# A fused AdaLN block of Mamba-style mixer and routed FFN: half of the next batch's z tiles ahead of the output products, first y statistics behind the state of chunk 6

## The reference, cut to what matters

```python
h = layernorm(x) * (1 + ca) + sa                  # per batch
# mixer, INNER = 512 channels, 8 heads, state 64
xi = silu(causal_conv4(h @ Wx.T));  z = h @ Wz.T
b, c, dt = xi @ Wb.T, xi @ Wc.T, softplus(xi @ Wdt.T + b_dt)
y = ssd_scan(xi, b, c, dt, a) + d * xi            # state carried over 1024 tokens
yn = groupnorm(y)                                 # mean and variance over all tokens of a head
x = x + ga * ((yn * silu(z)) @ Wout.T)            # "output products"
h = layernorm(x) * (1 + cb) + sb
# FFN: router weights h @ rw, the top 127 tokens are gathered, attention and MLP on them,
# scattered back; the others pass through
x = x + gb * ffn(h)
```

## Time and profile before

| | us |
|---|---|
| median of 3 runs | 1397.62 (1397.34 to 1399.22) |
| the profiled execution | 1401.03 |
| its span, first to last instruction | 1399.3 |
| TensorE busy | 1335.8 (95%) |
| VectorE busy | 945.3 (68%) |
| ScalarE busy | 685.8 (49%) |
| GpSimd busy | 351.8 (25%) |

### The profile page before, as it was taken

How to read it: one execution, slowest core, us unless ns; L and a number is a source line. 1 busy time by engine, 2 the same in 40 slices (tenths; PEclk the granted TensorE clock), 3 DMA queues, 4 the chain that set the end, 5 groups by cost and what they waited for, 6 DMA issues and landing times.

```text
span 1399.3 us, 26836 instructions
## 1 busy us (share of the span) xinstructions
PE 1335.8 (95%) x10517; PEld 827.2 (59%) x10531; DVE 945.3 (68%) x2649; ACT 685.8 (49%) x1351; POOL 351.8 (25%) x452
## 2 busy tenths in 40 slices
PE   8999999999999999999999999999999997999984
PEld 4447655586457665586456764576555863567543
DVE  2424797487874787567974878747875779746782
ACT  3534653754546562556436454466526554463312
POOL 3005301171105401072012611053010630134110
PEclk9999999999999999999999999999999998999997
DMA  8100001020000200020010200011000200101010
GB/s 278 45 0 32 9 23 49 1 82 31 27 23 8 75 31 27 23 81 18 14 49 1 82 31 27 23 33 50 30 27 23 81 24 8 49 3 50 31 49 4
DMA packets 47565, 54.47 MB, mean 39 GB/s; under 512 B 7624, under 2 KB 42312, under 8 KB 47440
## 3 DMA queue, kind: packets, MB, share of 16 engines
q1 hardware_dynamic: 41424, 46.41, 9.8%
q0 software_dynamic: 6016, 6.35, 1.7%
HBM read 34.84 MB, written 17.85 MB: 38 GB/s over the span
## 4 chain that ended last, share of the span: by engine, by line
PE 86%; DVE 6%; issue 4%; ACT 1%; DMA 1%; POOL 1%; POOLq 0%; DVEq 0%
PE ps L1576 46%; PE ps L1758 8%; PE ps L1655 4%; PE ps L1701 3%; PE ps L1898 2%; PE ps L1908 2%; PE ps L1667 2%; PE ps L1645 2%; PE ps L1716 1%; PE ps L1673 1%; PE ps L1863 1%; PE ps L1829 1%; PE ps L1684 1%; PE ps L1564 1%; PE ps L1594 1%
## 5 line engine op out<-in xcount | busy, mean ns | idle before, releaser
L1576 PE MATMUL ps<-xT,wb_s 128*128 128x512 f32 x512 | 233.7, 603 | 4.5 <-ACT xT L740 4.4
L1576 PE MATMUL ps<-xT,wc_s 128*128 128x512 f32 x512 | 225.4, 593 | 0.0
L1576 PEld LDWEIGHTS ps<-xT,wc_s 128*128 128x128 f32 x512 | 96.1, 190 | 112.3 <-issue 111.9
L1576 PEld LDWEIGHTS ps<-xT,wb_s 128*128 128x128 f32 x512 | 94.4, 192 | 114.4 <-issue 105.7
L1065 DVE SCALAR_TENSOR_TENSOR xT<-xc,cols_s,xT 128x512 f32<-128x512 f32 x192 | 134.8, 748 | 2.7
L1576 PE MATMUL ps<-hT,wx_s 128*128 128x512 f32 x256 | 117.6, 603 | 0.0
L1576 PE MATMUL ps<-hT,wz_s 128*128 128x512 f32 x256 | 113.8, 598 | 0.1
L1758 PE MATMUL ps<-CT,xT 128*128 128x256 f32 x512 | 111.9, 379 | 0.9 <-DVE xT L1239 0.9
L765 ACT ACTIVATE BT<-ps 128x512 f32<-128x512 f32 x64 | 37.9, 593 | 151.3 <-PE ps L1576 151.3
L1758 PEld LDWEIGHTS ps<-CT,xT 128*128 128x128 f32 x512 | 97.2, 190 | 17.8 <-issue 5.0
L1153 DVE TENSOR_TENSOR Mt<-ps,Eg 128x512 f32<-128x512 f32 x128 | 82.2, 684 | 26.5 <-PE ps L1701 26.5
(11 more groups left out here) (298 smaller groups left out, 2572.4 us busy)
## 6 DMA issues: line engine op xcount, KB each, us to landing
xr<-x SPq DMA_DIRECT2D x8, 1024.0 KB, 10.1
x_scratch<-xr SPq DMA_DIRECT2D x32, 256.0 KB, 2.1
out<-EC SPq DMA_DIRECT2D x32, 256.0 KB, 2.1
BT<-x SPq DMA_DIRECT2D x7, 1024.0 KB, 5.8
modrow<-mod_scratch SPq DMA_DIRECT2D x8, 512.0 KB, 7.0
w_s<-w SPq DMA_DIRECT2D x2, 1024.0 KB, 11.2
BT<-x SPq DMA_DIRECT2D x2, 512.0 KB, 5.4
xT<-wmod SPq DMA_DIRECT2D x1, 1024.0 KB, 9.7
```

What stands on the lines that cost most here:

```text
L1576: ins = t_.matmul(bank[:, :], w[:, k, m * P:(m + 1) * P], rhs[:, k, half * HALF:(half + 1) * HALF], start=k == 0, stop=k == nk - 1)
```

## The change

It has three parts.

- TensorE: the four z tiles of half 0 are issued ahead of `out_(f)` and not behind it. This alters the order for batches 1 to 6.
- ScalarE: the four SiLUs of these tiles are issued ahead of `last_tap(b, 0)`, in batches 0 to 6. In batches 1 to 6 each SiLU of a z tile also waits for the gating of batch b-1 that reads the same part of `zs`.
- VectorE: `y_stats(0, 0, 4)` is issued behind `state(6)` and `skip(6)`, in all eight batches.

```diff
@@ z_silu (ScalarE)
                     act.wait_ge(*proj.full(b, q))
+                    if later(b) and b < NB - 1:
+                        act.wait_ge(gd_ready, at(gd_ready, b - 1, half * KC + m + 1))
                     a.activation(zs[:, m, half * HALF:(half + 1) * HALF], proj.bank(q)[:, :], ACT.Silu
                                  ).then_inc(proj.drained[q % 4], 1)
@@ batch (ScalarE)
-                last_tap(b, 0)
                 if not last:
                     z_silu(b, 0, 0)
-                if not last:
                     z_silu(b, 0, 1)
+                last_tap(b, 0)
                 last_tap(b, 1)
@@ scan (VectorE)
-                    if c == 6:
-                        y_stats(0, 0, 4)
                     if c < T - 1:
                         state(c)
                     else:
                         y_stats(1, 4, 7)
                     skip(c)
+                    if c == 6:
+                        y_stats(0, 0, 4)
                 y_stats(2, 7, 8)
@@ batch (TensorE)
                 x_proj(b, 1, range(4))
                 if f is None:
                     pe.wait_ge(wload, 16 * len(first_loads))
+                if b < NB - 1:
+                    z_proj(b, 0, range(4))
                 if f is not None:
                     out_(f)
                 if b < NB - 1:
-                    z_proj(b, 0, range(4))
                     z_proj(b, 1, range(2))
```

## The result

| | before | after |
|---|---|---|
| median of the runs, us | 1397.62 (1396.32 to 1401.78, 5 runs) | 1432.01 (1429.99 to 1435.27, 5 runs) |
| profiled execution, us | 1401.03 | 1435.27 |
| its span, us | 1399.3 | 1433.5 |
| mean granted clock | 0.985 | 0.983 |

The ratio is 1.0248, 95% interval 1.023 to 1.0266: slower by 34.4 us. The forecast was 1431.4.

A forecast was written before the change was run, and what follows sets the result against it. TensorE was taken to bound the kernel, only 1.66 us above VectorE's chain. Terms 31.3 + 0.6 + 3.2 + 1.7 - 3.0 = +33.8 us on 1397.62 gave 1431.4 us; own range 1427 to 1436, widened to 1422 to 1441.

The forecast's parts named there:

- The floor of 28 us: Output products' end to first C tile: VectorE's chain, 27.99 us in batch 7, was claimed to set it in batches 1 to 6.
- +5.21 us for a batch: Batches 1 to 6: output products end 6.87 us later, the stretch behind them gets 1.66 shorter.
- 31.3 + 0.6: Batches 1 to 6 in all: +31.3 us for the moved z tiles, +0.6 for six bank waits.
- The bank wait: Second z tile reuses an x tile's bank that ScalarE must copy first: 0.1 us a batch, between 0 and 0.6.
- The four waits: TensorE behind the output products: router weights 0.5, first SiLU pair 0.5, B tile at k = 2 2.4, `ffn_idx` 1.4 us.
- no fall: TensorE's clock was taken to stay up behind the new waits, as these are shorter than batch 7's idle stretches.
- the clock rival: Clock falls behind the waits at `ffn_idx`, where nothing hides it: 1.8 us a batch, +10.8, 1442 us; chance 0.11.
- a fall at k = 2 alone: Half clock at the B tile would be hidden: batch 7 had it, 9.80 us against 8.85, within its 27.99.
- The y statistics: `gn_stats` waits for the later statistics, 0.45 us in each of seven batches (0.3 to 0.9): +3.2 us.
- the tail: After batch 7's scan, TensorE resumes 1.75 us earlier and its clock stays up: -3.0 us, between -1.75 and -3.1.
- Batch 0: ScalarE's SiLUs come ahead of the first tap, so the B tile resumes later: +1.7 us, between 0.5 and 3.
- the 0.83 us ahead of the first B tile: Weight load at k = 2 sat idle 0.83 us for ScalarE's last convolved-x SiLU, read as gated by VectorE's chain.

The follow-up runs named there:

- one_tile: Kernel before with one z tile and its SiLU ahead of the output products in batches 1 to 6; 1396.81 us against 1397.73, ratio 0.9993.
- two_tiles: Kernel before with two of the four z tiles and their SiLUs ahead of the output products in batches 1 to 6; 1408.62 us against 1397.73, ratio 1.0064.
- after_filled: Changed kernel with 16 extra products behind the router-weight transposes of batches 1 to 6; 1431.53 us against 1397.09 for the kernel before, ratio 1.0239.
- z_only: Kernel before with the TensorE and ScalarE parts of the change, y statistics left in place; 1432.59 us against 1397.73, ratio 1.0236.
- ystats_only: Kernel before with the VectorE part of the change alone (y statistics moved); 1397.78 us against 1397.73, ratio 1.001.
- before_filled: Kernel before with 16 extra products behind the router-weight transposes of batches 1 to 6; 1418.97 us, ratio 1.0154 to the kernel before.
- ystats_last: Kernel before with the y statistics of chunks 0 to 3 moved in the last batch alone; 1393.94 us against 1397.09, ratio 0.9983.
- silu_swap: ystats_last plus ScalarE's second convolved-x SiLU pair ahead of the last z SiLU pair, batches 1 to 6; 1392.99 us against 1398.28 (kernel before), ratio 0.9964.
- z_last_early: ystats_last plus batch 7's z tiles and SiLUs made as in other batches, dummy products in their old place; 1393.85 us against 1398.28 (kernel before), ratio 0.9968.
- both_early: The edits of silu_swap and z_last_early together; 1391.23 us against 1398.28 for the kernel before, ratio 0.9955.
- after_tap_out: Changed kernel without one tap of the convolution's first half (4 VectorE instructions a batch); 1410.46 us against 1397.09 for the kernel before, ratio 1.0093.

## Why the prediction was right

**The floor of 28 us.** This step carried the forecast and held: 28.01 us in three batches of the changed kernel (28.27 in the other three, see the clock below), 28.01 or 28.02 in all of one_tile, two_tiles and after_filled, and 2.90 less with 4 VectorE instructions fewer. Batch 7 had been a measurement of it, made by the kernel before itself.

**Its size.** Forecast +5.21 us for a batch. The profile says +7.18 in front, of which 0.1 is the statistics', and -1.64 or -1.37 behind. Without the statistics' part that is +5.4 or +5.7, and 33.4 for six batches, where the forecast had 31.3 + 0.6. The bank wait was 0.20, not 0.1. The four waits were put at 0.5, 0.5, 2.4 and 1.4; TensorE's idle was 0.58, 0.61, 2.18 and 1.26.

**The clock.** Here the forecast was half wrong. I took no fall. It fell in three of the six batches, behind the 2.2 us wait, and in three of six in z_only too: in batch 3 the same 20 pieces took 10.55 us in place of batch 2's 8.85.

```profile
536.51 10.55 PE L1577 MATMUL ps<-xT,wb_s 128*128 128x512 f32 x20 [2.17 <-ACT xT L740]
```

The windows after (stretch, length, busy by engine, granted clock, DMA), batch 2 first, then batch 3:

```profile
370.50:376.00 5.50, 5.50 (x14) 2.40 (x13) 5.50 (x16) 3.49 (x7) 0.00 (x0) 1.00 0.00 0
...
538.00:544.00 6.00, 6.00 (x12) 2.54 (x11) 6.00 (x19) 3.21 (x7) 0.00 (x0) 0.73 0.00 0
```

It cost 1.7 us of work and 0.26 us of time. VectorE's one-hot rows end 27.75 us behind the output products in batch 2 and in batch 3 alike, so the 1.26 us wait for them at `ffn_idx` took up most of the 1.7. In batch 3 that wait is nearly gone, and TensorE's own work comes last, by the 0.26. So the fall was nearly hidden, and the clock rival (+10.8), which has it where nothing hides it, stayed out. The prediction had said that a fall at k = 2 alone would be hidden.

The rule of the Trainium skill (TensorE: Matmul & The Clock Gate, "What's actually happening"), that recent activity releases the throttle, agrees with this trace in its direction: in batch 3 the granted clock was 1.00 up to the wait, 0.50 in 538 to 541 us, and 1.00 again from 542 us on, with TensorE at work all the while. It doesn't say why three batches were spared.

**The y statistics.** Forecast +3.2 in the stream and -3.0 at the tail. Measured: 0.4 a batch by ystats_only (2.8 in seven) and -3.16. The tail's number is right in part by luck. The prediction took the half clock behind the 2.96 us from one trace, as if it always came. It came in two of five profiles; only 1.53 of the 3.16 follows from the edit every time.

**Batch 0.** Forecast +1.7; 1.78 at the B tile. It can't be read from the first `gn_stats`. In the eight profiles whose kernels don't differ up to there (the kernel before, one_tile, two_tiles, before_filled, ystats_last, silu_swap, z_last_early, both_early) that mark stands anywhere from 153.7 to 157.6 us.

**What cancelled.** What follows from the change adds up to +36.6 us: 33.4 for the z tiles, 2.8 for the statistics, 1.8 for batch 0, -1.5 at the last `gn_stats` and 0.1 behind it. The spans of the two profiled executions differ by 34.2. The other -2.4 are in parts that vary by as much between kernels that don't differ there, so I count them as chance: 1.2 us less up to the first `gn_stats`, 1.9 less in the six scans, 1.6 less for the clock behind the 2.96 us, and 2.2 more in the last FFN, with 0.1 behind it. So it is partly luck that the sum came within 0.6 us: the z tiles were forecast 1.5 us too low, and the tail's gain was counted with a fall of the clock that doesn't always come. Of the 1.9 in the scans, 1.5 is shorter stops of TensorE for which the trace names no releaser (`issue`; those above 0.15 us are 3.4 us in sum before and 1.9 after).

**A step that was wrong without harm.** I read the 0.83 us ahead of the first B tile as a sign that VectorE's chain was close to binding there. before_filled and silu_swap show that it was ScalarE's order behind TensorE's own last z tile. VectorE's real distance was that of the whole stretch, 1.64 us, which I had from batch 7.

## What to carry to other kernels

Where one stage of a loop lacks a filler that the others have, its trace measures the other engine's chain: the work can be taken out of the others only until they are as short. Moving work from behind a producer to ahead of it costs its full length beyond that point, and gains nothing if no wait stood ahead of the producer. A wait that moves with the waiting engine's own work hides nothing, however long it is shown.

## What I had not expected of the hardware

- The clock fell behind an idle stretch of 2.2 us, with two of 0.6 us ahead of it in the same stretch, in three of six equal batches. In two_tiles, with two of the four tiles moved, the waits in batch 2 are 0.38 and 1.25 us and all six stretches were 28.01.
- Behind 2.96 us of idle in the tail the clock fell in two of five profiles. A cost that shows behind an idle stretch in one trace need not be there in the next.
- The time from the end of the last output products to the last FFN product has two sizes, with the same instructions: 68.7 to 68.8 us in six profiles (the kernel before, z_only, one_tile, after_tap_out, silu_swap, both_early) and 70.5 to 71.5 in the other seven. The windows show the granted clock at 0.50 for longer in the second kind. In the changed kernel, 52 us behind the products:

```profile
1401.36:1405.36 4.00, 3.22 (x37) 2.96 (x39) 0.29 (x1) 1.79 (x3) 0.00 (x0) 0.50 0.00 0
```

and the same stretch in the kernel before:

```profile
1369.38:1373.38 4.00, 2.83 (x41) 2.30 (x39) 0.32 (x1) 2.12 (x4) 0.00 (x0) 0.77 0.00 0
```

- From the last FFN product to the next `gn_stats`, in the six scans between batches 1 and 7, equal work took 42.05 to 44.01 us with the statistics in their old place, and 42.35 to 44.37 with them moved. The long ones are not those in which VectorE waits for the x load: with 0.82 us of that wait the kernel before took 42.06, its shortest, and with 0.18 us 43.73, its longest. What the longest has is a stop of TensorE in the middle of a group of 16 products (14 ahead, 2 behind) with nothing to wait for in the profile:

```profile
787.02 0.38 PE L1645 MATMUL ps<-EC,Sst 64*64 64x128 f32 x2 [1.30 <-issue]
```

  In 11 of the 13 profiles such a stop, of 0.76 to 1.65 us, stands in the fourth of the six scans. In the two kernels with extra products the fourth scan has none above 0.15 us, and one of 0.95 or 1.50 us stands in the fifth, there with VectorE's Mt named. What causes it was not tried.
